# Edge stage of a graph-attention layer: small tensors moved to PSUM, decays to SBUF, 28 of 64 columns fetched by TensorE in seven groups of four

## The reference, cut to what matters

```python
h = (x_flat @ W_gat).reshape(M, HEADS, NUM_EXPERTS)          # M = 16384 nodes, 4 heads of 4
a_src = (h * att_src).sum(-1)
a_dst = (h * att_dst).sum(-1)
e = leaky_relu(a_src[src] + a_dst[dst], negative_slope=0.2)  # 262144 edges, and one loop per node
e_max = segment_max(e, dst, num_segments=M)
ee = exp(e - e_max[dst])
denom = segment_sum(ee, dst, num_segments=M)
agg = segment_sum(h[src] * (ee / denom[dst])[:, :, None], dst, num_segments=M)
```

## Time and profile before

| | us |
|---|---|
| median of 3 runs | 6973.59 |
| lowest, highest | 6968.95, 6980.46 |
| profiled execution, its own time | 6982.49 |
| its span | 6980.8 |
| busy: PE, DVE, ACT, POOL | 5423.4, 5124.5, 2639.9, 2251.1 |
| edge stage: first row of it, last ACT row before the next stage | 3332, 5208 |

### The profile page before, as it was taken

One profiled execution on the slowest core, in us unless ns is written; L12 is line 12 of the kernel. 1 busy time (PEld: TensorE's weight loads), 2 busy tenths in 40 slices (PEclk: granted clock), 3 DMA queues, 4 the chain that ended last, 5 costly groups with the idle time before them and its releaser, 6 DMA issues. The chain is left out here.

```text
span 6980.8 us, 106469 instructions
## 1 busy us (share of the span) xinstructions
PE 5423.4 (78%) x40900; PEld 3371.2 (48%) x40900; DVE 5124.5 (73%) x8270; ACT 2639.9 (38%) x4182; POOL 2251.1 (32%) x2033
## 2 busy tenths in 40 slices
PE   5659879958739999970788888888850789689998
PEld 3552256632226666650666666666640258523332
DVE  7879987868878888860677777777761677677776
ACT  3434433434326666640333333333320332233332
POOL 0010010010037810006777777777767010100000
PEclk8879999979859999985899999999975889799999
DMA  0000000011111000000222221111111000100001
GB/s 16 1 6 1 25 17 21 10 27 45 55 32 14 20 2 2 2 33 12 38 37 37 37 37 37 37 37 37 37 25 12 1 3 3 17 1 1 1 1 25
DMA packets 146007, 138.98 MB, mean 20 GB/s; under 512 B 72162, under 2 KB 130180, under 8 KB 143812
## 3 DMA queue, kind: packets, MB, share of 16 engines
q1 hardware_dynamic: 89150, 112.03, 5.6%
q0 software_dynamic: 56448, 21.05, 3.7%
q10 hardware_dynamic: 12, 0.39, 0.0%
HBM read 60.64 MB, written 38.06 MB: 14 GB/s over the span
## 5 line engine op out<-in xcount | busy, mean ns | idle before, releaser
L2883 PE MATMUL edges_bank<-part_room,hot_room 128*128 128x512 f32 x6400 | 1539.2, 404 | 485.2 <-DVE hot_room L2956 484.3
L2883 PEld LDWEIGHTS edges_bank<-part_room,hot_room 128*128 128x128 f32 x6400 | 1249.6, 196 | 774.9 <-issue 493.1
L2871 POOL DMA_INDIRECT XT<-gat_node_table,edges_idx x1248 | 1477.8, 1184 | 381.5 <-issue 380.0
L2903 ACT COPY XT<-edges_bank 128x512 f32<-128x512 f32 x800 | 458.7, 594 | 1049.9 <-PE edges_bank L2883 1048.5
L2973 DVE COPY_PREDICATED XT<-edges_bits,XT 128x1280 f32<-128x1280 int32 (+3 forms) x640 | 566.9, 886 | 248.3 <-ACT XT L2903 224.5
L1005 ACT ACTIVATE expd_act_out<-expd_hp 128x1024 f32<-128x1024 f32 x256 | 261.9, 1023 | 526.2 <-PE expd_hp L927 526.2
L1041 DVE TENSOR_TENSOR expd_act_out<-expd_act_out,expd_h 128x1024 f32<-128x1024 f32 x256 | 312.7, 1221 | 185.9 <-ACT expd_act_out L1005 185.9
L1459 ACT ACTIVATE GT<-attc_sc,attc_nm 128x256 f32<-128x256 f32 x1024 | 399.6, 480 | 35.9 <-DVE attc_nm L1525 35.8
L1473 ACT ACTIVATE GT<-attc_sct 128x1024 f32<-128x1024 f32 x256 | 262.2, 1024 | 326.8 <-PE attc_sct L1393 326.6
L1524 DVE TENSOR_REDUCE attc_mx<-attc_sc 128x4 f32<-128x1024 f32 x256 | 313.4, 1224 | 86.2 <-PE attc_sc L1382 86.1
L2956 DVE TENSOR_SCALAR hot_room<-edges_lanes,edges_nodes 128x640 fp32r<-128x640 f16 x640 | 341.8, 594 | 0.1
(11 more groups left out here) (772 smaller groups left out, 9924.1 us busy)
## 6 DMA issues: line engine op xcount, KB each, us to landing
edges_lanes<-gat_places SPq DMA_DIRECT2D x160, 160.0 KB, 3.2
gat_states<-GT SPq DMA_DIRECT2D x32, 768.0 KB, 4.5
XT<-gat_node_table,edges_idx POOLq DMA_INDIRECT x1248, 2.6
XT<-XT SPq DMA_DIRECT2D x32, 256.0 KB
XT<-XT SPq DMA_DIRECT2D x64, 128.0 KB
XT<-XT SPq DMA_DIRECT2D x128, 64.0 KB
gat_starts<-nodes_zeros SPq DMA_DIRECT2D x4, 1088.0 KB, 8.1
attb_q<-attb_rows SPq DMA_DIRECT2D x256, 2.0 KB
```

The source lines that it names most:

```text
L2871: nc.gpsimd.indirect_dma_start(out=rows[:, k, c, :], out_offset=None, in_=q.t_table, in_offset=bass.IndirectOffsetOnAxis(ap=idx[:, k, c:c ...
L2883: m = nc.tensor.matmul(banks[t % BANKS][:], hot[:, (k * GROUPS + j) % 2, b, t, :], parts[:, p, b].rearrange("p c u -> p (c u)"), start=b = ...
L2903: nc.scalar.copy(fetched[:, (k * GROUPS + j) % 2, t].rearrange("p c u -> p (c u)"), banks[t % BANKS][:]).then_inc(fetched_in, 1)
```

## The change

The tile of the masks (`bits`), the reset mask, the keep mask and a copy of the attention vector go to one PSUM bank, the destinations' logits (`a_dst`) to a second, and a second copy of the weights, which ACT writes by an exponential of its own, to a third; L3019 reads the weights from there. The decays go to SBUF, `diff`, `inp_m` and `acc_m` to another place in SBUF. PE's columns go from 25 in 5 groups of 5 to 28 in 7 groups of 4, POOL's from 39 to 36, the banks for PE's columns from 5 to 4. `hot_room` is smaller accordingly.

```diff
--- before.py
+++ after.py
@@ -1068,7 +1068,7 @@
     g.part_room = nc.alloc_sbuf_tensor_at("part_room", [P, TOKENS // 4], F32R, offset=nc.sbuf_base - TOKENS * D * 4 // P)
     g.XT = sb("XT", [P, TOKENS])
     g.GT = sb("GT", [P, TOKENS], BF16)
-    g.hot_room = nc.alloc_sbuf_tensor_at("hot_room", [P, 5 * 1024], F32R, offset=nc.sbuf_base - 2 * TOKENS + 12 * 1024)
+    g.hot_room = nc.alloc_sbuf_tensor_at("hot_room", [P, 4 * 1024], F32R, offset=nc.sbuf_base - 2 * TOKENS + 12 * 1024)
     g.ident, g.ones = sb("ident", [P, P]), sb("ones", [P, P])
     g.identb = sb("identb", [P, P], BF16)
     g.stats = sb("stats", [P, TILES, 6])
@@ -2577,7 +2577,7 @@
 
 
 CHUNK = 64
-GROUPS, PER_GROUP = 5, 5
+GROUPS, PER_GROUP = 7, 4
 ON_PE = GROUPS * PER_GROUP
 BY_DMA = CHUNK - ON_PE
 CHUNKS = ROW // CHUNK
@@ -2779,23 +2779,25 @@
 
     C, W = CHUNK, CHUNK + 1
     NI = CHUNKS // 2
-    PARTS, BANKS = 2, 5
+    PARTS, BANKS = 2, 4
     LOW = LOW_PLACES
     WIDE = LOW * CH
     PERH = CH // HEADS2
     with Stage(nc, "edges") as st:
         starts = st.sb("starts", [P, 2, C, HEADS2])
         idx = st.sb("idx", [P, 2, C], I32)
-        inp_m, acc_m, reset = (st.sb(n, [P, HEADS2, W]) for n in ("inp_m", "acc_m", "reset"))
-        inp_s, acc_s = (st.sb(n, [P, HEADS2, 1 + PERH, W]) for n in ("inp_s", "acc_s"))
-        diff = st.sb("diff", [P, 2, HEADS2, C])
+        inp_s, acc_s, decay = (st.sb(n, [P, HEADS2, 1 + PERH, W]) for n in ("inp_s", "acc_s", "decay"))
         lanes = st.sb("lanes", [P, GROUPS, PER_GROUP, P], F16)
         att = st.sb("att", [P, CH])
         nodes_i, nodes = st.sb("nodes_i", [P, BLOCKS], I32), st.sb("nodes", [P, BLOCKS])
         pow2 = st.sb("pow2", [P, LOW_BITS], I32)
-        own_p = st.ps("own_p", [P, 3 * 512])
-        decay = own_p[:, 0:HEADS2 * (1 + PERH) * W].rearrange("p (h j t) -> p h j t", h=HEADS2, j=1 + PERH)
-        keep, bits = st.sb("keep", [P, C]), st.sb("bits", [P, LOW_BITS, ON_PE], I32)
+        tabs_p, weights_p, dst_p = (st.ps(n, [P, 512]) for n in ("tabs_p", "weights_p", "dst_p"))
+        reset = tabs_p[:, 0:HEADS2 * W].rearrange("p (h t) -> p h t", h=HEADS2)
+        keep, att_p = tabs_p[:, HEADS2 * W:HEADS2 * W + C], tabs_p[:, HEADS2 * W + C:HEADS2 * W + C + CH]
+        at = HEADS2 * W + C + CH
+        bits = tabs_p[:, at:at + LOW_BITS * ON_PE].bitcast(I32).rearrange("p (s t) -> p s t", s=LOW_BITS)
+        weights = weights_p[:, 0:HEADS2 * C].rearrange("p (h t) -> p h t", h=HEADS2)
+        a_dst = dst_p[:].rearrange("p (k h t) -> p k h t", k=2, h=HEADS2)
         state = g.GT[:].bitcast(F32)[:, 0:2 * C * ST].rearrange("p (k c r) -> p k c r", k=2, r=ST)
         hot = g.hot_room[:].rearrange("p (s b t e) -> p s b t e", s=2, b=BLOCKS, t=PER_GROUP)
         parts = g.part_room[:].rearrange("p (s b c u) -> p s b c u", s=PARTS, b=BLOCKS, c=CH)
@@ -2805,7 +2807,9 @@
         at = TOKENS // 2 + 2 * PER_GROUP * WIDE
         rows = g.XT[:, at:at + 2 * C * TAB].rearrange("p (k c r) -> p k c r", k=2, r=TAB)
         at += 2 * C * TAB
-        a_dst = g.XT[:, at:at + 2 * HEADS2 * C].rearrange("p (k h t) -> p k h t", k=2, h=HEADS2)
+        diff = g.XT[:, at:at + 2 * HEADS2 * C].rearrange("p (k h t) -> p k h t", k=2, h=HEADS2)
+        at += 2 * HEADS2 * C
+        inp_m, acc_m = (g.XT[:, at + n * HEADS2 * W:at + (n + 1) * HEADS2 * W].rearrange("p (h t) -> p h t", h=HEADS2) for n in range(2))
         places = q.t_place.rearrange("c e -> (c e)")
         banks = [st.ps(f"bank{m}", [P, WIDE]) for m in range(BANKS)]
         (split, numbered, powers, att_in, hot_ready, bank_full, fetched_in, halved, selected, pe_passed, act_passed, dve_passed) = (
@@ -2905,6 +2909,7 @@
 
                 def exps(c):
                     act.wait_ge(diff_ready, c + 1)
+                    nc.scalar.activation(weights, diff[:, 0], ACT.Exp)
                     nc.scalar.activation(inp_s[:, :, 0, 1:], diff[:, 0], ACT.Exp).then_inc(exped, 1)
                     nc.scalar.activation(decay[:, :, :, 1:], bc(diff[:, 1], 2, 1 + PERH), ACT.Exp).then_inc(exped, 1)
 
@@ -2948,7 +2953,7 @@
                 def low_bits(c):
 
                     at = src_row[:, ds(c * C + BY_DMA, ON_PE)]
-                    return vec.tensor_tensor(bits[:], bc(at, 1, LOW_BITS), bc(pow2[:], 2, ON_PE), ALU.bitwise_and)
+                    return vec.tensor_tensor(bits, bc(at, 1, LOW_BITS), bc(pow2[:], 2, ON_PE), ALU.bitwise_and)
 
                 def prepare(n, j, k):
                     v.wait_ge(lanes_in[j], 16 * n + 16)
@@ -2982,10 +2987,10 @@
                     link = chain(v, own, c, PER, 0)
                     now = q.keep[:, ds(c * C, C)]
                     vec.tensor_scalar(reset[:, :, 1:], bc(now, 1, HEADS2), -1.0, BIG, ALU.add, ALU.mult)
-                    link(vec.tensor_copy(keep[:], now))
+                    link(vec.tensor_copy(keep, now))
                     v.wait_ge(starts_in[k], 16 * i + 16)
                     for h in range(HEADS2):
-                        m = vec.tensor_tensor_scan(a_dst[:, k, h, :], keep[:], starts[:, k, :, h], a_dst[:, 1 - k, h, C - 1:C],
+                        m = vec.tensor_tensor_scan(a_dst[:, k, h, :], keep, starts[:, k, :, h], a_dst[:, 1 - k, h, C - 1:C],
                                                    ALU.mult, ALU.add)
                     m.then_inc(starts_used, 1)
                     v.wait_ge(starts_used, c + 1)
@@ -2995,7 +3000,7 @@
                     values = rows[:, k, BY_DMA:, 0:CH]
                     prod = inp_s[:, :, 1:, 1:1 + ON_PE].rearrange("p h e t -> p t h e")
                     link(vec.tensor_tensor(prod, values.rearrange("p t (h e) -> p t h e", h=HEADS2),
-                                           bc(att[:].rearrange("p (h e) -> p h e", h=HEADS2), 1, ON_PE), ALU.mult))
+                                           bc(att_p.rearrange("p (h e) -> p h e", h=HEADS2), 1, ON_PE), ALU.mult))
                     link(vec.reduce_sum(rows[:, k, BY_DMA:, CH:TAB], prod, AX.X))
                     v.wait_ge(gathered[k], 16 * BY_DMA * i + 16 * BY_DMA)
                     if more:
@@ -3005,8 +3010,8 @@
                     e = inp_m[:, :, 1:]
                     link(vec.tensor_tensor(e, rows[:, k, :, CH:TAB].rearrange("p t h -> p h t"), a_dst[:, k], ALU.add))
                     link(leaky(vec, e, e))
-                    link(vec.tensor_tensor_scan(acc_m[:].rearrange("p h t -> p (h t)"), reset[:].rearrange("p h t -> p (h t)"),
-                                                inp_m[:].rearrange("p h t -> p (h t)"), 0.0, ALU.add, ALU.max))
+                    link(vec.tensor_tensor_scan(acc_m.rearrange("p h t -> p (h t)"), reset.rearrange("p h t -> p (h t)"),
+                                                inp_m.rearrange("p h t -> p (h t)"), 0.0, ALU.add, ALU.max))
                     vec.tensor_tensor(diff[:, 0], e, acc_m[:, :, 1:], ALU.subtract)
                     link(vec.tensor_tensor(diff[:, 1], acc_m[:, :, 0:C], acc_m[:, :, 1:], ALU.subtract))
                     vec.scalar_tensor_tensor(diff[:, 1], diff[:, 1], 0.0, reset[:, :, 1:], ALU.min, ALU.add).then_inc(diff_ready, 1)
@@ -3016,9 +3021,9 @@
                     vec.tensor_copy(inp_s[:, :, :, 0], acc_s[:, :, :, C])
                     v.wait_ge(exped, 2 * c + 2)
                     values = rows[:, k, :, 0:CH].rearrange("p t (h e) -> p h e t", h=HEADS2)
-                    vec.tensor_tensor(inp_s[:, :, 1:, 1:], values, bc(inp_s[:, :, 0, 1:], 2, PERH), ALU.mult).then_inc(rows_used, 1)
+                    vec.tensor_tensor(inp_s[:, :, 1:, 1:], values, bc(weights, 2, PERH), ALU.mult).then_inc(rows_used, 1)
                     v.wait_ge(rows_used, c + 3)
-                    vec.tensor_tensor_scan(acc_s[:].rearrange("p h j t -> p (h j t)"), decay.rearrange("p h j t -> p (h j t)"),
+                    vec.tensor_tensor_scan(acc_s[:].rearrange("p h j t -> p (h j t)"), decay[:].rearrange("p h j t -> p (h j t)"),
                                            inp_s[:].rearrange("p h j t -> p (h j t)"), 0.0, ALU.mult, ALU.add).then_inc(sums_ready, 1)
                     v.wait_ge(sums_ready, c + 1)
 
@@ -3051,6 +3056,8 @@
                 v.wait_ge(cleared, 6)
                 v.wait_ge(split, 3)
                 v.wait_ge(att_in, 16)
+                vec.tensor_copy(att_p, att[:]).then_inc(cleared, 1)
+                v.wait_ge(cleared, 7)
                 prepare(0, 0, 0)
                 prepare(0, 1, 0)
                 for j in range(GROUPS):
```

## The result

| | us |
|---|---|
| median of 4 runs after | 7019.05 (7010.93 to 7022.01) |
| median of 4 runs before, same chip | 6973.79 (6968.95 to 6980.46) |
| ratio, 95% interval | 1.0062 (1.0045 to 1.008) |
| profiled execution after, its span | 7022.01, 7020.3 |

The change made the kernel slower by 45 us where 112 were forecast. The direction and the mechanism came as written: the gather left the path and the ring between PE and DVE (PE waits for the DVE's one-hots, the DVE for PE's columns, which ACT copies) took its place. Its length was overestimated, 61.2 us a chunk against 59.1.

The account below looks back on a forecast made before the run. The gather on POOL bounds, 58.0 us a chunk; then a PE-DVE loop of 60.3 plus 0.9 clock loss, 61.2. Periods +116, ahead +4, behind -8.5: +112 on 6973.6 gives 7085 us; range 7000 to 7125.

Parts of the forecast that it names:

- the ring between PE and DVE: PE only two groups ahead, waiting for DVE's prepare: 51.6 us a chunk before, 60.3 after, 61.2 with clock loss.
- only the gather mattered: Rival: without the gather wait the chunk falls to the DVE's own 52.1 us, total 6804 us; chance 0.03.
- the operands in PSUM make the DVE fast: Rival: selects, L3019, L2997 and L3006 get shorter, chunk 56.9 us, total 6952 us; chance 0.06.
- the port is not freed: Rival: gathers stay held, POOL up to 59.3 us but under the PE-DVE loop, total 7057 to 7114; chance 0.04.
- The variant with the selects' fixed part alone: Only the masked copies' fixed time falls: chunk 59.1 us, total 7021; faster selects (7000 to 7040) had chance 0.04.
- Select and prepare, three times 5.55: DVE's select and prepare, three times in the PE-DVE loop: 6.45 us before, 5.55 each after.
- a fifth less of all of it would be -0.44, none -0; I take -0.27: DVE's prepare, 2.20 us for four comparisons of 640 elements: saves 0.27 us with smaller groups, bounds 0 and 0.44.
- I take half of the chunks: +0.9.: PE's clock falls at group 3 after 1.8 us idle, costing 1.84 us, in half the chunks: +0.9 us a chunk.
- ahead of the first maxima: Before the first period: three more columns 5.5 us, less 1.4 for shorter select and prepares, plus 0.2: +4 us.
- from the last maxima to the next stage: Stage end: the 9.3 us gather wait goes, less 0.8 for larger steps: -8.5 us.
- 31 periods: From first to last maxima: 1781.1 us before, 31 x 61.2 = 1897 after, +116 us.
- If nothing were freed: POOL's gathers per chunk if the operand moves free no port: 58 to 59.3 us, against 49 us when freed.

Follow-up runs that it names:

- sbuf28: Kernel before with 28 columns in seven groups of four and four banks, all operands where they were; 7022.29 us, ratio 1.0071.
- out2: Kernel after with two extra unread 1024-element DVE products per chunk, behind select and prepare of group 3, outside the PE-DVE loop; 7032.02 us, one run.
- in2: Kernel after with two extra unread 1024-element DVE products per chunk, behind the sums, inside the PE-DVE loop; 7167.64 us, one run.
- cols25: Kernel after with 25 columns in five groups of five and five banks again, moved operands kept, inp_m and acc_m in SBUF tiles of their own; 6789.4 us, ratio 0.9738.
- in1: Kernel after with one extra unread 1024-element DVE product per chunk, behind the sums, inside the PE-DVE loop; 7081.86 us, one run.

## Why the prediction was right in direction and wrong in size

**Right.** The gather sets the pace before, a ring closes behind it, and two groups of four are less cover than two of five. The ring's sum with the measured pieces of DVE and PE, and 0.74 and 0.36 as forecast, is 0.74 + 15.63 + 7.71 + 5.49 + 0.36 + 16 x 1.826 (29.2) = 59.1, against 59.09. sbuf28 shows that 28 columns in groups of four make it, out2 against in2 that it is the ring. The rival "only the gather mattered" falls with in2 and after; "the operands in PSUM make the DVE fast" with L3024 at 2.27 us and the masked copies at 1289 ns against 1288; "the port is not freed" with 0.94 us under the masked copies. The variant with the selects' fixed part alone was priced at 59.1 us and 7021, which is what came out, but for another reason: sbuf28 has it without a moved operand. That agreement is luck.

**Wrong: two terms of the ring.** The forecast period was 61.2, 2.1 too long; the two terms below are 1.9 of it.

*Select and prepare, three times 5.55.* Measured are 5.15 to 5.25, 1.0 us less a chunk, 32 us in all. The select was sized right (3.69 forecast, 3.57 to 3.66 measured). The step that failed is "a fifth less of all of it would be -0.44, none -0; I take -0.27": the prepare went from 2.12 us elapsed to 1.59, outside both bounds. The bounds scaled the four comparisons' joint time of 2.20 us by their count of elements, as if all of it were the comparisons' own. The rows of the comparison before, in sbuf28 and in the kernel after (min, median, max in ns):

```profile
L2956 DVE TENSOR_SCALAR hot_room<-edges_lanes,edges_nodes x640: 534/549/774, 3342.2 to 5163.0; 128x640 fp32r<-128x640 f16 x160
```

```profile
L2956 DVE TENSOR_SCALAR hot_room<-edges_lanes,edges_nodes x896: 473/480/487, 3332.8 to 5218.2; 128x512 fp32r<-128x512 f16 x180
...
L2961 DVE TENSOR_SCALAR hot_room<-edges_lanes,edges_nodes x896: 466/480/694, 3339.0 to 5219.4; 128x512 fp32r<-128x512 f16 x180
```

The medians differ by 13%, the longest by far more. What makes them long is POOL. Two comparisons of the kernel before, at 4041.42 (547 ns) and 4041.88 (766 ns), and the gather beside them:

```profile
L2956 DVE TENSOR_SCALAR hot_room<-edges_lanes,edges_nodes x2: 547/656/766, 4041.4 to 4041.9; 128x640 fp32r<-128x640 f16 x2
...
4041.30 1.03 POOL L2871 DMA_INDIRECT XT<-gat_node_table,edges_idx  x1 [0.30 <-issue]
```

The gather ends at 4042.33 and the second comparison at 4042.65. In the kernel before 114 of the 640 comparisons took 757 to 774 ns. Every one of them began 0.44 to 0.46 us ahead of a gather's end and ended 0.31 to 0.32 us behind it, and none of the others took over 600. In the kernel after the comparisons that began 0.29 to 0.44 us ahead of a gather's end ended 0.24 to 0.25 us behind it, 43 of 896, and while POOL stood idle for its buffer none took over 487. In sbuf28, with the operands where they were, none of the 896 began in that stretch, and none was long; in cols25, with the masks in PSUM, 119 of 640 did and were. So it is neither the operands' place nor the elements alone, but when a comparison begins against the gather. This is read from the times, no run was made for it.

Four comparisons without a held one took 1.95 to 1.99 us at 640 elements and 1.66 to 1.69 at 512: the elements are worth some -0.3, close to the -0.27 taken. What the step had wrong is the other 0.2 to 0.25 of the 2.20 us, which was waiting for POOL. In the kernel before each of the 31 chunks had at least one held prepare among its three in the ring (18 had three), in the kernel after none had.

*"I take half of the chunks: +0.9."* In the kernel after the clock fell at group 3 in none: 0, which is 28 us. The second wait was 0.55 to 1.70 us, 1.13 in the mean. The prediction's own terms, 5.49 + 5.55 - (7.3 + 1.84), make 1.90 and not the 1.8 it wrote. Of the difference 0.3 is the shorter select and prepare, and the larger part, 0.46, is group 2, which took 9.60 us in the mean and not 9.14. So the wait lay below the 1.88 us of the earlier trace rows that did bring the clock down. in1 and in2 show the mechanism at work once the wait is longer. That it would take half of the chunks was a guess between two rows from other stages, and it should have carried a lower chance.

The other terms: ahead of the first maxima +1.0 (forecast +4; over the runs here that point lies anywhere from 3391.9 to 3414.3 us, so that this term says little); from the last maxima to the next stage 31.54 us before and 22.60 after, -8.9 (-8.5); 31 periods +50.7 (+116). That makes +42.8, and 3.3 us come back in later stages, which the change doesn't touch: 39.5 between the two spans. Against the medians it is 45.

**Also off, at no cost.** "If nothing were freed" POOL was put at 58 to 59.3 us; sbuf28 measures 52.4. A group's delay there is (52.4 - 45.0)/7 = 1.06 us and not 1.3 to 1.5, and the sums hold almost nothing, since POOL mostly idles under them: 4 gathers in the whole stage ended with the hold by the product, where the kernel before has 31.

What the moved operands alone were worth could have been read before: at 25 columns the ring was 51.6 us and the gather 58.0, so that they could bring about 6 us a chunk. That is cols25.

## What to carry to other kernels

When a wait goes, close the next loop from the trace before pricing the change: here it ran through three handovers, PE to ACT to DVE and back to PE, and its cover was the number of columns in two groups, which the same change made smaller. One edit of the pair was worth -184 us by itself and the other took it all back; edits that come together are priced apart, each against the bound that is left. A joint time of several instructions is not scaled by elements before its single durations have been read, and a long one is set beside what the other engines do at that moment.

## What the runs showed of the hardware

- A one-hot comparison (fp16 in, fp32r out) of 640 elements takes 549 ns in the median and up to 774; of 512 elements 480 and at most 487 in sbuf28, 694 in the kernel after. The long ones began 0.3 to 0.5 us ahead of the end of a gather on POOL and ended 0.31 us (640 elements) or 0.25 us (512) behind it, in 114 of 640 before, 43 of 896 after, 0 of 896 in sbuf28. Four in a row take 1.95 to 1.99 us and 1.67 when none is held, 2.20 with a held one of 640.
- A gather's descriptors took 0.94 us under a product with one operand in PSUM, 2.61 with both in SBUF, and 2.86 and 3.01 in the chunks shown under the scan once its decays were in SBUF. A held gather ended 0.75 to 0.76 us behind the DVE instruction that held it: 31 of 31 under the product before, 30 of 30 under the scan after.
- The clock of PE behind a short wait does not follow from its length alone: in in1, in front of the same group, 1.84 to 2.11 us brought it down each time (12), 1.67 to 1.78 (3) and 2.17 to 2.92 us (14) never, 3.00 us once. The group in front of a shorter wait had run longer at the lower clock. Why was not tried.
- Writing the reset mask to PSUM took 0.42 us against 0.29 to SBUF.
